# A decoder layer on one core: the first loads in another order, and the gate weights folded ahead of the first turning

## The reference, cut to what matters

```python
x = x + _L0_attn_ref(_layernorm(x), Wq, Wk, Wv, Wo, gw, sw)      # gated linear attention, 16 heads
x = x + _L0_xattn_ref(_layernorm(x), ctx, ctx, igate_w, ..., rpe, ln_w, ln_b, hops)   # mLSTM, 8 heads
x = x + _L0_ffn_ref(_layernorm(x), ..., router_w, w1, b1, w2, b2)  # 8 experts, 2 for each token

# the first part
Q, K, V = x @ Wq.T, x @ Wk.T, x @ Wv.T
g = clip(sigmoid(x_heads @ gw.T), 1e-6)
Gc = exp(clip(cumsum(log(g)), -30, 30)) + 1e-6
R = silu(K_heads @ sw.T)
S = cumsum(outer(K, V) * R / Gc) * Gc
out = (Q applied to S) @ Wo.T
```

## Time and profile before

| | us |
|---|---|
| median of three runs | 844.79 |
| lowest, highest | 840.76, 845.15 |
| the profiled execution | 838.66 |
| its span, first to last instruction | 836.9 |

### The profile page before, as it was taken

The page is one execution under the profiler, slowest core; times in us unless marked ns, Lnnn a source line. Parts: engine busy times, 40 slices in busy tenths (PEclk is TensorE's granted clock), DMA queues, the critical chain, the costliest instruction groups (busy, mean ns, idle before and its releaser), DMA issues.

```text
span 836.9 us, 17067 instructions
## 1 busy us (share of the span) xinstructions
PE 751.9 (90%) x5866; PEld 662.0 (79%) x5867; DVE 403.1 (48%) x966; ACT 353.4 (42%) x916; POOL 429.7 (51%) x504
## 2 busy tenths in 40 slices
PE   7888888878988888898798887999999999999996
PEld 5566666657888878897787775689999999999995
DVE  2456666555554433332569897723333333333331
ACT  1333333324555433332667754144444444444441
POOL 6566666656666666666445541124444444444442
PEclk8999999989999999999889999999999999999999
DMA  9233333343233336356267699322221222122221
GB/s 293 78 102 103 109 113 111 111 121 93 84 92 89 89 89 189 89 108 194 83 185 202 201 282 354 120 77 38 38 38 32 37 38 38 31 38 38 38 36 22
DMA packets 75812, 88.29 MB, mean 106 GB/s; under 512 B 11952, under 2 KB 66032, under 8 KB 75632
## 3 DMA queue, kind: packets, MB, share of 16 engines
q0 software_dynamic: 19824, 43.93, 21.1%
q1 hardware_dynamic: 52256, 40.12, 16.5%
q10 hardware_dynamic: 3680, 3.54, 1.2%
HBM read 75.83 MB, written 11.73 MB: 105 GB/s over the span
## 4 chain that ended last, share of the span: by engine, by line
PE 40%; issue 27%; POOL 14%; DVE 9%; ACT 5%; another core or an unknown queue 3%; DMA 1%; POOLq 1%; DVEq 0%; ACTq 0%
PE ps L1964 15%; POOL out L1660 7%; PE ps L1030 7%; POOL G L1640 5%; PE ps L484 3%; PE ps L525 2%; PE ps L551 2%; DVE U L809 1%; ACT G L1353 1%; DMA out<-G,slots 1%; PE ps L1227 1%; PE ps L1673 1%; PE ps L592 1%; PE ps L477 1%
## 5 line engine op out<-in xcount | busy, mean ns | idle before, releaser
L331 POOL DMA_INDIRECT G<-in_rpe,hopi x193 | 186.6, 967 | 108.2 <-issue 42.1
L1756 ACT ACTIVATE G<-ps,U 128x128 f32<-128x128 f32 x312 | 84.9, 382 | 160.5 <-PE ps L1705 160.5
L1705 PEld LDWEIGHTS ps<-G,QT 128*128 128x128 f32 x1248 | 145.2, 192 | 1.9
L1705 PE MATMUL ps<-G,QT 128*128 128x128 f32 x1248 | 145.5, 275 | 0.0
L1713 PE MATMUL ps<-G 128*128 x624 | 141.2, 379 | 1.3 <-DVE G L1900 1.3
L1713 PEld LDWEIGHTS ps<-G 128*128 128x128 f32 x624 | 115.5, 190 | 15.8 <-issue 1.7
L1964 PE MATMUL ps<-U,PET 128*128 128x128 f32 (+3 forms) x768 | 104.2, 275 | 9.1 <-issue 8.7
L1964 PEld LDWEIGHTS ps<-U,PET 128*128 128x128 f32 x768 | 94.7, 192 | 14.6 <-issue 14.2
L978 DVE COPY PET<-ps 128x512 f32<-128x512 f32 x64 | 44.1, 690 | 116.1 <-PE ps L1030 99.3
L2007 ACT ACTIVATE PET<-ps 128x512 f32<-128x512 f32 (+1 forms) x63 | 37.4, 594 | 113.3 <-PE ps L1030 83.3
L1660 POOL DMA_INDIRECT out<-G,slots x39 | 66.7, 1711 | 24.4 <-issue 24.4
(11 more groups left out here) (241 smaller groups left out, 1239.7 us busy)
## 6 DMA issues: line engine op xcount, KB each, us to landing
G<-run_max SPq DMA_DIRECT2D x16, 512.0 KB, 6.4
U<-in_w SPq DMA_DIRECT2D x16, 512.0 KB, 7.2
G<-in_w SPq DMA_DIRECT2D x8, 1024.0 KB, 10.2
G<-in_rpe,hopi POOLq DMA_INDIRECT x193
U<-in_ctx SPq DMA_DIRECT2D x8, 256.0 KB
tokens_kept<-X SPq DMA_DIRECT2D x8, 256.0 KB
X<-tokens_kept SPq DMA_DIRECT2D x1, 2048.0 KB
hidden_rows<-QT ACTq DMA_DIRECT2D x8, 256.0 KB, 7.4
```

Of the source, the lines that this page charges most:

```text
L331: pool.indirect_dma_start(out=dst, out_offset=None, in_=rpe_d, in_offset=bass.IndirectOffsetOnAxis(ap=hopi[:, n:n + 1], axis=0)) \
L1705: mm = pe.matmul(bank(1 + 2 * u + c // 4, 4, P)[:, c % 4], w1c[u][:, k, c], hT[u][:, k, :], start=(k == 0), stop=(k == KC - 1))
L1756: ins = nc.scalar.activation(gel[u][:, c, :], bank(1 + 2 * u + c // 4, 4, P)[:, c % 4], ACT.Gelu, bias=b1c[u][:, c:c + 1])
```

## The change

SP's first transfers are cut and put in another order. Only sequence 0 is behind `ld_x`. The columns of the constants are renumbered, so that the table can be loaded in three pieces: identity, head masks and parities (144 columns, `ld_cst`); triangles, ones and block mask (512 columns, a new semaphore `ld_tri`); the rest (520 columns, on `ld_lnb`, behind `lnbb`). The indices stand fifth. Sequence 1 is put on `ld_g`, ahead of the gate weights. VectorE builds `swb` and the gate columns before it norms sequence 0, and takes the statistics of sequence 1 behind `ld_g`. ScalarE computes the inverse deviation of sequence 1 between the two copies of values. TensorE folds the gate weights first and turns sequence 0 behind that; two fillers are gone (one of 512 columns, one of 256).

```diff
-            sp.dma_start(hopi[:, :], idx_d).then_inc(ld_idx, 16)
-            sp.dma_start(X[:, 0:4], x_d[0:2].rearrange("b (c p) d -> p (b c) d", p=P)).then_inc(ld_x, 16)
-            sp.dma_start(cst[:, :], cst_d).then_inc(ld_cst, 16)
+            tokens(0, 1, ld_x)
+            constants_of(C_ID, C_TRI, ld_cst)
             sp.dma_start(gwc, gw_d).then_inc(ld_s, 16)
             sp.dma_start(swc, sw_d).then_inc(ld_s, 16)
+            sp.dma_start(hopi[:, :], idx_d).then_inc(ld_idx, 16)
+            constants_of(C_TRI, C_IOTA, ld_tri)
+            tokens(1, 2, ld_g)
             sp.dma_start(wg6, wg_d.rearrange("(k p) n -> p k n", p=P)).then_inc(ld_g, 16)
             sp.dma_start(gbias, gb_d.partition_broadcast(P)).then_inc(ld_g, 16)
             sp.dma_start(lnbb, lnb_d.partition_broadcast(P)).then_inc(ld_lnb, 16)
-            sp.dma_start(X[:, 4:T], x_d[2:B].rearrange("b (c p) d -> p (b c) d", p=P)).then_inc(ld_xr, 16)
+            constants_of(C_IOTA, C_W, ld_lnb)
+            tokens(2, B, ld_xr)
...
             pe.wait_ge(zeros, 1)
-            for n in (512, 512, 512, 256):
+            for n in (512, 512, 256):
                 keep_going(n, nil, 6)
-            pe.wait_ge(ld_cst, 16)
...
                 mm.then_inc(w_full, 1)
-                pe.wait_ge(w_ready, 2)
...
             def cum(b):
                 pe.wait_ge(lg_r, b + 1)
                 pe.wait_ge(kk_r, b + 1)
+                if b == 0:
+                    pe.wait_ge(ld_tri, 16)
...
+                if b < 0:
+                    fold_weights()
+                    pe.wait_ge(ld_cst, 16)
                 if new:
                     tokens_turned(b + 1)
                 if b < 0:
                     keep_going(256, nil, 6)
-                    fold_weights()
-                    keep_going(256, nil, 6)
+                    pe.wait_ge(w_ready, 2)
...
             inv_std(rstd[0], mv[0][:, :, 1], mv_r, 1, rstd_r)
-            inv_std(rstd[1], mv[1][:, :, 1], mv_r, 2, rstd_r)
...
                 if new:
                     values(b + 1, 0)
+                if b < 0:
+                    inv_std(rstd[1], mv[1][:, :, 1], mv_r, 2, rstd_r)
...
             dve.wait_ge(ld_x, 16)
-            for b in range(2):
-                stats(b, st[b], mv[b], mv_r)
-            norm(0, xna, mv[0], rstd[0], rstd_r, xn_r)
+            stats(0, st[0], mv[0], mv_r)
             dve.wait_ge(ld_cst, 16)
             dve.wait_ge(ld_s, 32)
             nc.vector.tensor_scalar(swb, hm16, swc, None, ALU.mult).then_inc(w_ready, 1)
             dve.wait_ge(ch_v, 1)
             for k in range(KC):
                 nc.vector.tensor_scalar(wvx[:, k, D + k * HC:D + (k + 1) * HC], hm16, gwc, None, ALU.mult)
+            norm(0, xna, mv[0], rstd[0], rstd_r, xn_r)
             dve.wait_ge(w_full, 1)
             nc.vector.tensor_copy(wvx[:, :, D + HA:D + 2 * HA], bank(0, KC, HA)).then_inc(w_ready, 1)
-            dve.wait_ge(ld_g, 32)
+            dve.wait_ge(ld_g, 48)
+            stats(1, st[1], mv[1], mv_r)
...
-                        dve.wait_ge(ld_lnb, 16)
+                        dve.wait_ge(ld_lnb, 32)
```

More of the change, by code:

```diff
@@ L25 @@
 MLSTM_EPS = 1e-6
-C_ID, C_TRI, C_TRIREV, C_ONE, C_BLK = 0, 128, 256, 384, 512
-C_HM16, C_HM32, C_IOTA = 640, 648, 652
-C_TOK, C_CNT, C_TILE, C_RESET, C_PAR, C_CENT, C_PAD = 660, 692, 708, 748, 876, 878, 1006
-C_POS, C_SLOT, C_W = 1007, 1135, 1174
+C_ID, C_HM16, C_HM32, C_PAR, C_TRI, C_TRIREV, C_ONE, C_BLK = 0, 128, 136, 140, 144, 272, 400, 528
+C_IOTA, C_TOK, C_CNT, C_TILE, C_RESET, C_CENT, C_PAD = 656, 664, 696, 712, 752, 880, 1008
+C_POS, C_SLOT, C_W = 1009, 1137, 1176
 NT = 2 * B * S // P + E * (P - 1) // P
@@ L253, in build @@
         ld_wv, ld_wq, ld_wkT, ld_wo, zeros = sem("ld_wv"), sem("ld_wq"), sem("ld_wkT"), sem("ld_wo"), sem("zeros")
-        ld_wk, ld_s, ld_g = sem("ld_wk"), sem("ld_s"), sem("ld_g")
+        ld_wk, ld_s, ld_g, ld_tri = sem("ld_wk"), sem("ld_s"), sem("ld_g"), sem("ld_tri")
         w_ready, w_full = sem("w_ready"), sem("w_full")
@@ L335, in tokens_sync, with tokens, constants_of @@
         def tokens_sync(sp):
-            sp.dma_start(hopi[:, :], idx_d).then_inc(ld_idx, 16)
-            sp.dma_start(X[:, 0:4], x_d[0:2].rearrange("b (c p) d -> p (b c) d", p=P)).then_inc(ld_x, 16)
-            sp.dma_start(cst[:, :], cst_d).then_inc(ld_cst, 16)
+            def tokens(b0, b1, landed):
+                sp.dma_start(X[:, 2 * b0:2 * b1], x_d[b0:b1].rearrange("b (c p) d -> p (b c) d", p=P)).then_inc(landed, 16)
+            def constants_of(c0, c1, landed):
+                sp.dma_start(cst[:, c0:c1], cst_d[:, c0:c1]).then_inc(landed, 16)
+            tokens(0, 1, ld_x)
+            constants_of(C_ID, C_TRI, ld_cst)
             sp.dma_start(gwc, gw_d).then_inc(ld_s, 16)
             sp.dma_start(swc, sw_d).then_inc(ld_s, 16)
+            sp.dma_start(hopi[:, :], idx_d).then_inc(ld_idx, 16)
+            constants_of(C_TRI, C_IOTA, ld_tri)
+            tokens(1, 2, ld_g)
             sp.dma_start(wg6, wg_d.rearrange("(k p) n -> p k n", p=P)).then_inc(ld_g, 16)
```

## The result

| | before | after |
|---|---|---|
| median of six runs, us | 844.97 | 852.97 |
| lowest, highest | 840.76, 848.28 | 848.65, 854.04 |
| the profiled execution | 838.66 | 848.65 |
| its span, its mean granted clock | 836.9, 0.977 | 846.9, 0.962 |

The ratio is 1.0093, with a 95% interval from 1.0065 to 1.0121: the change makes the kernel slower by nearly 1%, and the forecast of 840.0 was wrong in its sign.

A forecast was written before the change was run, and what follows sets the result against it. The start was taken as bound by the SP queue's order; vectors' path (queries at 13.5 to 15.6) and second sequence's (15.1) gave 15.2 for 18.77, gain 3.6. Profiled 838.66 became 835.1; median forecast 840.0, range 835.5 to 844.5.

The forecast's parts named there:

- First statistics: VectorE's statistics of the first sequence: start at about 4.0 in place of 6.36, hidden by the wait for the vectors.
- Arrival of the vectors: Gate vectors on SP's queue: landing at 6.5 in place of 10.5, gain 4.0, from 2.6 to 4.9.
- 2.2 us of it again: Vectors' tail behind the constants on SP's queue: 2.2 us as before (8.3 to 10.5), giving 6.1, taken as 6.5.
- Rival 4: Gate vectors' 4-byte rows take their own long time anywhere, landing at 9 or later; gain 1.5 or less, 842.2; chance 0.05.
- The fold ahead of the first turning: TensorE from vectors' arrival to first value matmul: 3.65 to 4.65 us, 3.8 before; first value at 10.15 to 11.15.
- The second sequence: New wait shared with the gate weights: statistics from 13.0 put queries at 15.1; from 12.0, 14.1; from 14.5, 16.6.
- The queries: TensorE's start of the queries: 15.2 in place of 18.77, gain 3.6 us, bounds 2.2 (16.6) and 4.7 (14.1).
- What is moved at no cost: Loads issued later: indices' first gather at about 7.2, 3.5 later, lag gone by some 60 us through GpSimd's waits.
- Without that cover it would be 3.5: GpSimd's gathers: the cost in us of their later start if its waits for TensorE did not absorb the lag.
- The shift at 60 us is the shift at the queries: Every event behind the queries comes 3.6 us earlier; a different shift at 60 us would make the prediction wrong.
- Rival 2: TensorE's clock stays low through the work behind the queries: to 31 it costs 10 us, time 850; chance 0.05.
- The Trainium skill's rule: SP's loads: transfers under 64 KB are mostly overhead; three more would put an estimated 6 us before the last, no gain.

The follow-up runs named there:

- e16: Kernel before with the two small gate vectors issued second, behind the indices and ahead of the tokens; ratio 1.0045, on the chip without late completions.
- e13: Changed kernel with ten plain transfers on SP's queue in place of GpSimd's ten opening gathers; ratio 1.0010 to the kernel before, on the chip without late completions.
- e14: Kernel before with ten plain transfers on SP's queue in place of GpSimd's ten opening gathers; ratio 0.9988, on the chip without late completions.
- e17: Changed kernel itself run again, on a chip of the usual kind; ratio 1.0102 to the kernel before.
- e2: Changed kernel with TensorE's and VectorE's work ahead of the first pass in the order of before, new transfers kept; ratio 1.0111 to the kernel before.
- e18: Kernel before itself run again, for a trace on one chip with the changed kernel; ratio 1.0012.
- e15: Kernel before with 14 opening gathers in place of 10; ratio 0.9944, on the chip without late completions.
- e9: Changed kernel with two gathers at once in place of ten, the other eight spread over passes 1 to 6; ratio 1.0166 to the kernel before.
- e10: Kernel before with two gathers at once in place of ten, the other eight spread over passes 1 to 6; ratio 1.0169.
- e7: Kernel before with only the indices moved from first to fifth place, behind the gate vectors; ratio 1.0114.
- e3: Changed kernel with the indices issued first again; ratio 1.0030 to the kernel before.
- e4: Changed kernel with its two removed fillers put back; ratio 1.0091 to the kernel before.
- e6: Changed kernel with two gathers issued at once in place of ten, the other eight left to the next stage; ratio 1.0090 to the kernel before.
- e1: Changed kernel with the transfers of the kernel before, only the order of the work new; ratio 1.0014 to the kernel before.
- e12: Changed kernel whose first 15 gathers fetch rows for 32 of 128 partitions; a single execution, 846.78 us, 1.0036 times the kernel before.
- e5: Changed kernel in which GpSimd waits for the first cumulative sum before its first gather; ratio 1.0244 to the kernel before.

## Why the prediction was wrong

- *First statistics* at 4.0: 4.13. Right.
- *Arrival of the vectors* at 6.5, bounds 5.6 and 7.9: 8.73, outside the bounds. They were issued at 1.75 and 2.22, so it took them 6.5. The step that failed is the tail of "2.2 us of it again": the rows of before gave the time in which nothing else was left to move (445 packets, 8.3 to 10.5), not what 256 rows of 4 bytes cost a queue. e16 measured that: 3 to 4 us. Rival 4 (they take their own long time, "land at 9 or later") is nearly what happened. e13 and e14 have no gathers there, and the vectors landed at about 8.0 and 10.1: the gathers, the reason for the lower bound, matter little.
- *The fold ahead of the first turning*: forecast 3.65 to 4.65 from the vectors to the first value; measured 3.96 (8.84 to 12.80). Right, and at the low clock: fold 1.85, turning 1.09 (1.11 at the low level in the earlier trace rows, 0.63 at the high one in the earlier trace rows). The trace of the changed kernel has no record of the clock there; e17, the same kernel, has 0.56 and 0.50 with the same 1.85 and 1.09. One term of the forecast's lower end was too large: 1.84 for the fold is its low-clock time, and at the full clock it takes 1.03 (e2, e14).
- *The second sequence*, "from 13.0": 12.86. Right. The wait is no bound: the copy behind it came at 16.36, right behind its matmuls.
- *The queries* at 15.2: 16.82, a gain of 1.95 in place of 3.6, just outside the bound of 16.6. The vectors came 2.2 later than forecast, and a clock that was back at 14.0 in place of 17.4 made up for a part. But the size of this miss is not settled: against e18, e17 gains 3.27. The same order of loads and of work ahead of the queries gave starts from 15.82 (e14, clock never low) to 20.48 (e15, low from 9.0 to 19.2) in the kernel before, though in these two the early gathers differ too.
- *"What is moved at no cost"*: this step turned the sign. The indices were put down as 3.5 later (7.2) and free, because GpSimd's waits for TensorE (11.2 us in 13 waits) would take up the lag. First the size: 9.99, 6.3 later, behind the vectors' rows, which now stand ahead of the indices. Then the mechanism, in two parts. The waits were no slack of GpSimd's: e9 and e10 gave it extra gathers in the passes that hold those waits, and each cost 1.5 to 2.9 us. And the opening gathers, which lay beside filler and waiting up to 19.9 before, now ran until 28.7, over keys, scores and cumulative sum, where TensorE has its first unbroken work: there they met the late completions, 4.5 and 5.9 us. e7 alone has the whole loss from this step, and e3 gives most of it back. "Without that cover it would be 3.5" was low too: it is 10.
- *"The shift at 60 us is the shift at the queries"*: it was -1.95 at the queries and +8.6 at the first projection; the prediction named this as what would make it wrong.
- *The rivals.* Rival 2, slower by a low clock behind the queries, gave 850 and came nearest in time. But its mechanism is a consequence (some 3 of the 8.6 us at the first projection): the clock fell behind a rest of TensorE that it did not cause, filler doesn't help (e4), and e6 keeps the clock at 1.00 from 20.5 to 32 and is as slow at the end. None of the rivals had the gathers in it.
- *The Trainium skill's rule* ("DMA: Bandwidth & Descriptors", "Rules for kernel authors": coalesce small transfers) was weighed by the number of transfers, three more, and that is not what it cost: e2 has them all and its vectors are used at 9.22, 1.4 earlier than before. Where the trace agrees with the page is the two vectors that were small already; e16 shows their price.

The third of the loss that e3 doesn't give back, 1.0030 [1.0004, 1.0056], may be e1's 1.0014: in both the turning stands behind the fold and the queries come at 21.2, later than before. It is too near to no change to be settled.

**What stays open.** Why TensorE's signals are late and its matmuls crawl while GpSimd issues gathers, and why not on one chip of the four that these batches used. The bytes of the gathers are excluded (e12); a low clock for want of filler is, too (e4, e6). The Trainium skill, "DMA: Bandwidth & Descriptors", section "Latency and other measured facts", names a shared port between the descriptor rings of GpSimd's transfers and two of the DMA engines as a best guess for those engines being slow; no run here shows a port, and the page has nothing on TensorE's signals. Both kernels on the chip without late completions, with traces, would tell whether the change costs anything there; e13 and e14 are the nearest, and they show no gain.

## What to carry to other kernels

An engine's waits in a trace are slack only if more work put into them costs nothing; before a load is moved later because "its reader waits anyway", price the reader's whole list, and what its work will fall beside once it is late. In this kernel the first load had to be that of the engine with the longest list to issue behind it, not that of the engine that needs its data first. And a load of many tiny rows is paid by everything that is queued behind it: put it last, or try a queue of its own, which no run here did.

## What the hardware did that was not expected

- A completion of TensorE reached ScalarE 4.5 us (keys, changed kernel) to 22.2 us (queries, e5: 34.56 to 56.79) behind the modelled end of its matmul, while GpSimd issued gathers one behind the other; in the later passes of both kernels ScalarE waits up to 3.7 for one. On one chip it didn't happen, and there the kernel before took 784.5 us in place of 839 to 845. Nearly the whole difference lies in the stages that gather: products end at 353.1 (e15) against 406.7.
- 256 rows of 4 bytes, 1 KB in all, held back by 3 to 4 us what stood behind them in their queue.
- SP's own issues were held: 1.76 and 1.41 us for the gate weights and their bias, where the kernel before has 0.50 and 0.62.
- The low clock at the start lay elsewhere in two traces of the kernel before: 10.5 to 17.4 and, in e18, 11.3 to 18.1; their queries start at 18.77 and 19.93. In its variants with other early gathers it was 12.0 to 15.4 (e10, queries 17.77) or absent (e14, 15.82). So a microsecond between two single traces of the start need not come from the change.
